# Twelve-head graph layers: the destination row is added inside PSUM by a K=3 bf16 matmul

## The reference, cut to what matters

```python
z   = (x @ W).reshape(N, 12, 64)
el  = sum(z * attn_l, axis=-1);  er = sum(z * attn_r, axis=-1)
e   = leaky_relu(el[src] + er[dst], 0.2)
ex  = exp(e - segment_max(e, dst)[dst])
out = segment_sum(ex / segment_sum(ex, dst)[dst] * z[src], dst) + z + bias
```

## Time and profile before

| what | value |
|---|---|
| runs | 3783.88 us median of 3 (3781.05, 3783.88, 3795.34) |
| span of the profiled execution | 3780.9 us |
| its own time | not listed apart; the fastest run, 3781.05 us, is 0.15 us above the span |
| PE busy, DVE busy, ACT busy | 2914.6 us (77%), 1979.8 us (52%), 1219.4 us (32%) |
| blocks of layer 0 | from 354.4 us to 825.3 us |
| blocks of layer 1 | from 1003.0 us to 1478.4 us |

### The profile page before, as it was taken

One profiled execution on the slowest core, in us unless ns is written; L12 is line 12 of the kernel. 1 busy time (PEld: TensorE's weight loads), 2 busy tenths in 40 slices (PEclk: granted clock), 3 DMA queues, 4 the chain that ended last, 5 costly groups with the idle time before them and its releaser, 6 DMA issues.

```text
span 3780.9 us, 46025 instructions
## 1 busy us (share of the span) xinstructions
PE 2914.6 (77%) x14456; PEld 2141.7 (57%) x14457; DVE 1979.8 (52%) x3392; ACT 1219.4 (32%) x1944; POOL 235.8 (6%) x267
## 2 busy tenths in 40 slices
PE   6874999978499996849369269649995994945995
PEld 4542888864288886425257124238884552534773
DVE  6745999945699984551431234556641434233113
ACT  1122778842277774230024101133320222001110
POOL 0000000000000000000001300000000000000112
PEclk9987999989799998979569679869997997965996
DMA  1011121121111212001335621122222100123435
GB/s 61 0 45 46 51 66 55 57 61 34 45 60 54 67 44 62 33 28 29 122 111 196 184 102 60 62 94 78 71 64 96 44 33 20 31 95 110 163 128 168
DMA packets 102475, 276.89 MB, mean 73 GB/s; under 512 B 25358, under 2 KB 38104, under 8 KB 99115
## 3 DMA queue, kind: packets, MB, share of 16 engines
q1 hardware_dynamic: 66794, 194.26, 14.1%
q0 software_dynamic: 32976, 73.59, 7.5%
q10 hardware_dynamic: 2600, 7.68, 0.5%
HBM read 204.99 MB, written 72.91 MB: 74 GB/s over the span
## 4 chain that ended last, share of the span: by engine, by line
PE 42%; DMA 13%; DVE 6%; issue 2%; ACT 1%; SPq 1%; POOL 1%; ACTq 0%; DVEq 0%; POOLq 0%
PE psum L914 16%; PE psum L870 12%; DMA arena<-raw 6%; PE psum L1032 4%; PE psum L1041 4%; PE psum L941 3%; DMA arena<-y_rows,arena 2%; PE psum L931 2%; DVE arena L1460 1%; DMA arena<-r_rows 1%; DMA arena<-xn_rows,arena 1%; PE psum L860 1%; DMA arena<-x 1%; DVE arena L1488 1%; DMA arena<-el_rows 1%
## 5 line engine op out<-in xcount | busy, mean ns | idle before, releaser
L914 PE MATMUL psum<-arena 125*125 125x256 f32 (+3 forms) x2400 | 626.1, 421 | 84.6 <-DVE arena L1490 84.6
L870 PE MATMUL psum<-arena 128*125 128x384 f32 (+1 forms) x1840 | 663.2, 520 | 0.0
L941 PEld LDWEIGHTS psum<-arena 125*125 125x125 f32 x4800 | 580.3, 191 | 71.7 <-DVE arena L1485 16.7
L914 PEld LDWEIGHTS psum<-arena 125*125 125x125 f32 x2400 | 449.5, 189 | 256.3 <-issue 66.9
L941 PE MATMUL psum<-arena 125*125 (+1 forms) x4800 | 568.3, 271 | 16.7 <-DVE arena L1485 16.6
L870 PEld LDWEIGHTS psum<-arena 128*125 128x125 f32 x1840 | 347.6, 191 | 291.2 <-issue 121.9
L1460 DVE CUSTOM_DVE_ANT_0 arena<-arena,no_edge_bias 125x1250 bf16<-125x1250 f32 x300 | 436.5, 1455 | 79.7 <-DMA arena<-el_rows 73.1
L931 PE MATMUL psum<-arena,spread 126*125 126x313 f32 (+1 forms) x1344 | 437.7, 449 | 33.4 <-DMA arena<-r_rows 18.7
L1485 DVE SCALAR_TENSOR_TENSOR arena<-arena,edge_counts 125x625 f32<-125x625 f32 x480 | 381.9, 805 | 79.5 <-ACT arena L1200 79.3
L1187 ACT ACTIVATE arena<-arena,el 125x625 f32<-125x625 f32 x480 | 386.4, 806 | 38.4 <-DMA arena<-el_rows 38.4
L1200 ACT ACTIVATE arena<-psum,el 125x625 f32<-125x625 f32 x336 | 262.6, 782 | 200.9 <-PE psum L931 179.2
(11 more groups left out here) (192 smaller groups left out, 2631.8 us busy)
## 6 DMA issues: line engine op xcount, KB each, us to landing
arena<-el_rows SPq DMA_DIRECT2D x54, 610.4 KB
arena<-in_L_ffn_W SPq DMA_DIRECT2D x16, 1152.0 KB, 9.1
y_rows<-arena SPq DMA_DIRECT2D x47, 384.0 KB, 2.4
arena<-raw SPq DMA_DIRECT2D x40, 375.0 KB
arena<-r_rows SPq DMA_DIRECT2D x24, 610.4 KB
arena<-in_L_w SPq DMA_DIRECT2D x16, 768.0 KB, 6.2
arena<-in_L_gnn_W SPq DMA_DIRECT2D x4, 3072.0 KB, 12.7
z_heads<-arena POOLq DMA_DIRECT2D x10, 1000.0 KB, 12.3
```

Of the source, the lines that this page charges most:

```text
L870: ins = e.matmul(bank[0:P, 0:w], L.xt[u][:, k, :], L.w_sb[:, k, at:at + w], start=(k == 0), stop=(k == L.KT - 1))
L914: ins = e.matmul(banks[2 + 2 * (j % 2) + c][0:P, 0:w], Ph[half][:, s, d * P:(d + 1) * P], (L.zh[u] if L.spill else L.z)[:, s, at:at + w], ...
L941: ins = e.matmul(banks[2 + half][0:P, d * 65:(d + 1) * 65], Ph[half][:, s, d * P:(d + 1) * P], L.z[:, s, h, :], start=(s == 0), stop=(s == ...
```

## The change

In the twelve-head layers:

- `relu` writes its block straight into PSUM (`block_exponents(j)`) for all 20 blocks, two blocks ahead instead of three; it waits until the exponential of block j - 2, ACT's own previous instruction but for a possible row copy, has finished, since there are only two such places.
- `exponents` adds the row to it there, `start=False`, with `ones3` (3 x 125, bf16) as the weights and three rows of bf16 as the moving side: the destination row is split into three bf16 parts whose sum is the f32 value. All 20 blocks go this way.
- `add_r2`, `rb2`, `r2`, `spread` and their semaphores go. `max_end` makes the three parts: seven small instructions in place of two. The transpose and the copy handle 30 columns instead of 20.
- SP's `lay_r3` writes the 30 x 125 bf16 rows to DRAM and reads them back as three rows (7.5 KB), where `lay_r2` had a 610 KB broadcast and six small reads. `load_el` follows directly.
- Four matmuls per layer write once over the four banks before the first block (`primed`).

```diff
-ADD_AT = [3, 7, 9]
...
-        spread = sb("spread", [P + 1, P])
+        ones3 = sb("ones3", [3, P], BF16)
+        r_part = sb("r_part", [P, 2 * 3 * T])
+        r_bf = sb("r_bf", [P, 2 * T], BF16)
...
-            def lay_r2(h, u, i, first, more):
+            def lay_r3(h, u, i):
 
                 e.wait_ge(L.rt_sb, L.since["rt_sb"] + h + 1)
                 apart(e)
-                e.dma_start(r_rows[h, T:2 * T, :], L.rt[u][T:2 * T, :]).then_inc(L.r_out[u], 16)
+                e.dma_start(r3_rows[h, :, :], L.rt3[u]).then_inc(L.r_out[u], 16)
                 e.wait_ge(L.r_out[u], L.since["r_out"][u] + 16 * (i + 1))
                 apart(e)
                 if not isinstance(i, int) or i > 0:
-                    e.wait_ge(L.added, L.since["added"] + ADDS * (h - 1))
+                    e.wait_ge(L.t_ready, L.since["t_ready"] + 2 * T * (h - 1))
                     apart(e)
-                e.dma_start(L.rb2[u], over(r_rows[h, T:2 * T, :].rearrange("t p -> (t p)"))).then_inc(L.rb2_in[u], 16)
-                for half in range(2):
-                    if not first:
-                        e.wait_ge(L.t_ready, L.since["t_ready"] + TURNS * (h - 1) + TURNS // 2 * (half + 1))
-                        apart(e)
-                    for v in range(3):
-                        e.dma_start(L.r2[half][P:P + 1, v, :],
-                                    r_rows[h, T + half * HT:T + (half + 1) * HT, :].rearrange("(o t) p -> o (t p)", o=1)
-                                    ).then_inc(L.r2_in[half], 16)
-                    if half == 0 and more:
-                        load_el(h + 2, u)
+                e.dma_start(L.r3[u], r3_rows[h, :, :].rearrange("(j t) p -> j (t p)", j=3)).then_inc(L.r3_in[u], 16)
...
                 def rows_of(h, u, i, more):
...
                     load_er(h, u)
-                    lay_r2(h, u, i, False, more)
+                    lay_r3(h, u, i)
+                    if more:
+                        load_el(h + 2, u)
...
-            def exponents(h, j):
+            def exponents(h, u, i, j):
 
                 half, s = j // T, j % T
-                if s == 0:
-                    e.wait_ge(L.r2_in[half], L.since["r2_in"][half] + 48 * (h + 1))
+                if j == 0:
+                    e.wait_ge(L.r3_in[u], L.since["r3_in"][u] + 16 * (i + 1))
                 e.wait_ge(L.relued, L.since["relued"] + 2 * T * h + j + 1)
-                e.wait_ge(L.e_ready, L.since["e_ready"] + 2 * T * h + j + 1)
                 o = block_exponents(j)
                 for at, to in ((0, CUT), (CUT, HALF)):
-                    ins = e.matmul(o[:, at:to], spread[:, :], L.r2[half][:, s % 3, at:to], start=True, stop=True)
+                    ins = e.matmul(o[:, at:to], ones3[:, :], L.r3[u][:, half * HALF + at:half * HALF + to],
+                                   start=False, stop=True, skip_group_check=True)
                 ins.then_inc(L.t_ready, 1)
...
-                    if s not in ADD_AT:
-                        exponents(h, j)
+                    exponents(h, u, i, j)
...
+            if L.batched:
+
+                for b in range(4, 8):
+                    ins = e.matmul(banks[b][0:P, 0:512], noti[:, :], MB[:, 0, 0:512], start=True, stop=True)
+                ins.then_inc(L.primed, 1)
...
-
+                e.wait_ge(L.e_ready, L.since["e_ready"] + 2 * T * h + j + 1)
                 apart(e)
-                e.activation(L.r2[half][0:P, s % 3, :], L.erb[u][:, half * HALF:(half + 1) * HALF], ACT.Relu,
+                e.activation(block_exponents(j), L.erb[u][:, half * HALF:(half + 1) * HALF], ACT.Relu,
                              bias=L.el8[:, s, bass.ds(h, 1)], scale=1.0 - SLOPE).then_inc(L.relued, 1)
...
-                e.activation(L.ex[j % 4], src, ACT.Exp, bias=L.el2[:, s, bass.ds(h, 1)]).then_inc(L.e_ready, 1)
+                e.activation(L.ex[j % 4], block_exponents(j), ACT.Exp, bias=L.el2[:, s, bass.ds(h, 1)]).then_inc(L.e_ready, 1)
...
-                    if j + 3 < 2 * T:
-                        relu(h, u, i, j + 3)
+                    if j + 2 < 2 * T:
+                        relu(h, u, i, j + 2)
...
+                if L.batched:
+                    q = r_part[:, u * 3 * T:(u + 1) * 3 * T].rearrange("p (j t) -> p j t", j=3)
+                    st.add(e.scalar_tensor_tensor(out=v[0], in0=er, scalar=SLOPE, in1=v[1], op0=ALU.mult, op1=ALU.subtract))
+                    st.wait()
+                    st.add(e.tensor_copy(r_bf[:, 0:T], v[0]))
+                    st.wait()
+                    st.add(e.tensor_copy(q[:, 0, :], r_bf[:, 0:T]))
+                    st.add(e.tensor_tensor(v[1], v[0], r_bf[:, 0:T], ALU.subtract))
+                    st.wait()
+                    st.add(e.tensor_copy(r_bf[:, T:2 * T], v[1]))
+                    st.wait()
+                    st.add(e.tensor_copy(q[:, 1, :], r_bf[:, T:2 * T]))
+                    e.tensor_tensor(q[:, 2, :], v[1], r_bf[:, T:2 * T], ALU.subtract).then_inc(L.r_ready, 1)
+                    return
                 st.add(e.tensor_tensor(r[:, 0:T], er, v[1], ALU.subtract))
...
-            def add_r2(h, u, i, j):
...
-                    if j + 3 < 2 * T and (j + 3) % T in ADD_AT:
-                        add_r2(h, u, i, j + 3)
```

More of the change, by code:

```diff
@@ L38 @@
 BAL_EPS = 0.01
-ADD_AT = [3, 7, 9]
-ADDS, TURNS = 2 * len(ADD_AT), 2 * (T - len(ADD_AT))
-def of_vector(j):
-    return sum(v % T in ADD_AT for v in range(j))
 def split(total, parts):
@@ L113, in __init__ @@
             elb_in=[16 * n for n in of], r_ready=heads, rt_ready=heads, rt_sb=heads, r_out=[16 * n for n in of],
-            rb_in=[16 * n * (not self.batched) for n in of], relued=2 * T * heads * self.batched, t_ready=TURNS * heads * self.batched,
-            added=ADDS * heads * self.batched, rb2_in=[16 * n * self.batched for n in of],
-            er_in=[16 * n * self.batched for n in of], r2_in=[48 * heads * self.batched] * 2, z_in=[16 * n * spill for n in of], e_ready=2 * T * heads, e_free=2 * T * heads * (not self.batched),
+            rb_in=[16 * n * (not self.batched) for n in of], primed=1 * self.batched, relued=2 * T * heads * self.batched, t_ready=2 * T * heads * self.batched,
+            er_in=[16 * n * self.batched for n in of], r3_in=[16 * n * self.batched for n in of], z_in=[16 * n * spill for n in of], e_ready=2 * T * heads, e_free=2 * T * heads * (not self.batched),
             p_ready=2 * T * heads, p_free=2 * heads, ag_ready=banks, out_done=banks, stored=[8 * banks] * 2)
@@ L128, in __init__ @@
         self.t_ready = signals["t_ready"]
-        self.added = signals["added"]
-        self.rb2_in = signals["rb2_in"]
+        self.primed = signals["primed"]
         self.er_in = signals["er_in"]
-        self.r2_in = signals["r2_in"]
+        self.r3_in = signals["r3_in"]
         self.x_in = signals["x_in"]
@@ L342, in graph_transformer @@
                 at += 2 * N
-                L.r2 = [carve(at + half * 3 * HALF, P + 1, 3 * HALF).rearrange("p (u d) -> p u d", u=3) for half in range(2)]
-                at += 6 * HALF
+                L.r3 = [carve(at + u * HALF, 3, HALF).bitcast(BF16) for u in range(2)]
+                at += 2 * HALF
                 L.ex = [carve(at + u * HALF, P, HALF) for u in range(4)]
@@ L348, in graph_transformer @@
                 at += 4 * HALF
-                L.rb2 = [carve(at + u * N, P, N) for u in range(2)]
-                at += 2 * N
+                L.rt3 = [carve(at + u * 63, 3 * T, 63).bitcast(BF16)[:, 0:P] for u in range(2)]
+                at += 126
             else:
@@ L569, in gat_sync @@
                 load_er(1, 1)
-                lay_r2(0, 0, 0, True, True)
-                lay_r2(1, 1, 0, False, True)
+                lay_r3(0, 0, 0)
+                load_el(2, 0)
+                lay_r3(1, 1, 0)
+                load_el(3, 1)
                 def rows_of(h, u, i, more):
@@ L945, in sum_tile, with batched_head @@
                     e.matmul(banks[1][0:1, 0:1], ident[:, 0:1], ident[:, 0:1], start=True, stop=True).then_inc(L.p_free, 1)
-            def batched_head(h, u, first, last):
+            def batched_head(h, u, i, first, last):
                 for j in range(2 * T):
                     half, s = j // T, j % T
-                    if s not in ADD_AT:
-                        exponents(h, j)
+                    exponents(h, u, i, j)
                     if not (first and half == 0):
@@ L1165, in rows @@
                 e.wait_ge(L.rt_ready, L.since["rt_ready"] + h + 1)
+                if L.batched:
+                    e.activation(L.rt3[u], banks[0][0:3 * T, 0:P], ACT.Copy).then_inc(L.rt_sb, 1)
+                    return
                 e.activation(L.rt[u], banks[0][0:2 * T, 0:P], ACT.Copy).then_inc(L.rt_sb, 1)
@@ L1206, in batched_head @@
                         rows(h + 1, 1 - u)
-                    if j + 3 < 2 * T:
-                        relu(h, u, i, j + 3)
+                    if j + 2 < 2 * T:
+                        relu(h, u, i, j + 2)
                     elif not last:
```

(15 more changed lines are left out.)

32 lines of the change are left out of this document (14 added, 18 removed).

## The result

The changed kernel takes **4306.48 us** (median of 4 runs, 4300.79 to 4311.25). The kernel before took 3786.35 beside it (4 runs, 3781.05 to 3795.34). The ratio is 1.136, with a 95% interval of 1.1333 to 1.1386: 13.6% slower where I forecast 3% faster. The profiled execution has a span of 4301.7 us, 520.8 above that of before.

The account below looks back on a forecast made before the run. The prediction took PE (37.2 us a head) as the bound, DVE close behind at 36.5; savings of 59 us per layer, 118 for two, less 7 in reserve, gave 3780.9 - 111 = 3669.9, so 3672 us, range 3648 to 3722.

Parts of the forecast that it names:

- the granted clock: PE in the twelve-head layers: clock 1.00 from head 1 on, so PE needs 28.4 us a head, behind DVE's 33.1.
- the rival on the other side: PE's new rests drop its clock to 1.2 GHz: 56.8 us a head, some 4200 us; 6% to end slower.
- The sign that I had named for it: Rows of L941, the sums, at 2.1 us in the middle of a layer would show the prediction wrong.
- A low clock makes PE the bound again, so its rests vanish: Argument against the low-clock rival: PE at the low level would set the pace and no longer rest.
- The window that was busy for 88% at 1.00: Argument against the low clock: the projection's window, PE busy 17.60 of 20 us, was granted 1.00 throughout.
- the 11.13 us of L941 alone: Argument against the low clock: at a layer's end, sums alone kept 0.11 us an instruction over 11 us.
- PE's pair: Per block on PE: two K=3 bf16 matmuls adding the row take 0.33 us beside sums of 1.07.
- ACT's wait on itself: Per block on ACT: the rectifier waits for the exponential just before it, 0.17 us more, block 1.55, head 31.3.
- ACT becomes the bound: Rival: ACT's wait of 0.35 us a block makes heads 34.9 us, 3719 us in all; 16% for 3692 to 3765.
- DVE and the heads: DVE sets heads 1 to 9 at 33.1 us, its 1.36 us wait for `el` gone; 0.3 per head kept back.
- The start: Layer start: row's write to first exponential takes 5.2 us, not 12.8; 6.6 us saved, head 0 another 3.4.
- The sum: Both layers: 59 us saved in each, 118, less 7 kept back, 111; forecast 3672 us, 3.0% less.

Follow-up runs that it names:

- e2: The changed kernel with the row matmul in f32 instead of bf16, still over 3 rows: 5076.27 us.
- e6: The changed kernel with extra unread matmuls of 3 rows, 512 columns, in head 0 of each layer, as many as in e3: 4374.3 us.
- e5: The changed kernel with the row matmul in f32 and over 125 rows, weights zero below the third: 3906.34 us.
- e3: The changed kernel with extra unread bf16 matmuls of 125 rows in head 0, eight for each of its first ten blocks, three for each of the last: 4294.18 us.
- e1: The changed kernel with the bf16 row matmul over 125 rows instead of 3, weights zero below the third: 4093.22 us.
- e4: The changed kernel, 3-row pairs kept, with two extra unread 125-row bf16 matmuls per block in all heads: 4643.84 us.
- f3: f1 with the row matmul left at 3 rows, same extra matmuls: 4314.18 us.
- f1: e1 plus extra 125-row matmuls: head 0 filled as in e3, 18 in head 1's first block, 8 at each later half: 3671.87 us, ratio 0.9715 to the kernel before.
- e12: e9 with the row matmul over 3 rows instead of 125: 3797.33 us.
- e9: e1 plus extra 125-row matmuls: e3's fill of head 0, 18 in head 1's first block, 5 at each half, 1 per other block: 3687.12 us.
- f2: f1 without the eight extra matmuls at each half from head 1 on: 4033.25 us.
- e7: e1 with e3's fill of head 0 and one extra 125-row matmul per block from head 1 on: 4272.94 us.
- e8: e1 with e3's fill of head 0 and no extra matmul from head 1 on: 4091.21 us.

## Why the prediction was wrong

**The step that failed is the granted clock.** The forecast priced PE at the full level, 28.4 us a head, and so put DVE in front; PE was at the low level in all of both layers' heads behind the first, took 60.45 us a head and set the time. I had this as the rival on the other side and gave it 6%. Its sum came close: 56.8 us a head and some 4200, measured 60.45 and 4306. The sign that I had named for it, sums of 2.1 us and more in the middle of a layer, is there (2.36 for ten at 625.65). Two arguments against it were wrong.

- "A low clock makes PE the bound again, so its rests vanish": they did vanish, and it changed nothing. PE was busy for 660 of 660 us at 0.50. Being busy isn't what brings the clock up; e2 and e6 are busy without a rest on 3 rows and stay low, e5 and e3 with 125 rows rise. That some full rows are there isn't enough either (e1, e4).
- The window that was busy for 88% at 1.00 and the 11.13 us of L941 alone were both of matmuls with 125 rows. They show such work at the full level. They say nothing of 3 rows, or of the way up. The same hundred sums alone, met at the low level, stayed there; timeline of PE in the changed kernel, end of layer 1:

```profile
1976.41 21.26 PE L928 MATMUL psum<-arena 125*125 125x65 f32 x100
```

The row that did bear on the way up was in the trace: the f32 L931 of 126 rows in head 0 (2.29 us, then 1.27).

The Trainium skill's section that I weighed, "A second HAM failure mode: psum-queue depth-cycling" in "TensorE: Matmul & The Clock Gate", expects a pace between the levels, up and down. The changed kernel doesn't go up and down: it is low for all of both layers. Only f3 alternates, and without any idle time of PE.

The other terms, read in the changed kernel and in f1, where the clock is full:

- **PE's pair.** I took 0.33 us beside ten sums of 1.07. At full clock a block with 3 rows is 401.54 - 399.90 = 1.64 us, not 1.40; with 125 rows it is 1.31 (f1, 621.67 to 622.98). A pair of 3 rows is 0.41 and delays the loads behind it. The bounds of a head (21.8 to 33.8) held it: 20 x 1.64 + 0.4 is 33.2. So even at full clock the 3-row form would have put PE level with DVE; that is an estimate from these rows, as no run has the 3-row form at full clock through a layer without an extra matmul per block. At the low level a block is 3.00 instead of 2 x 1.40 = 2.80; twenty times 0.20 is 4.0 us, and the head is 3.65 above my 56.8.
- **ACT's wait on itself.** Exponential to rectifier is 0.85 to 0.93 us (743.50 to 744.35 in f1, 370.39 to 371.31 above) where I had 0.84; rectifier to exponential is 0.73. Where ACT alone sets the pace in f1 its block is 744.35 - 742.77 = 1.58 (I had 1.55). The rival "ACT becomes the bound" didn't come about, though ACT (324.09 us busy) now stands beside DVE (321.24) in the window of f1.
- **DVE and the heads.** In f1 nine heads take (721.47 - 415.63) / 9 = 33.98 us, against 33.1 and the 0.3 kept back. Between 430 and 720 us DVE has no wait for `el`, and waits for ACT for 13.5 us in 22 places, about 1.6 a head, which neither list of mine held.
- **The start.** 5.27 us from write to first exponential, forecast 5.2. In f1 head 1's `turn_r` comes 425.88 - 415.63 = 10.25 us earlier than in the earlier trace rows, forecast 6.6 + 3.4 = 10.0.
- **The sum.** f1 takes 3671.87 us where I forecast 3672. Part of that is chance: f1 has padded rows and extra matmuls that my sum didn't. It shows that the relief of DVE and PE was there to be had with padded rows. From f1 to the changed kernel is 635 us. The clock is most of it but not all: at the same full clock 3 rows cost 110 us more than 125 (e12 - e9), so the forecast time isn't shown for the change as it was made.

**What stays open.** Whether the pause of 1.11 us or the thinner work cost f2 its clock, when the kernel before kept it behind pauses of 1.09 and 2.26 us. Whether it is the count of rows filled or a count of something that goes with it, as the zero weights below row 3 already suffice (e5); counts between 3 and 125 weren't tried. Which of f1's extra matmuls could still go; for the extra matmuls of a half only 0 (f2) and 8 were tried without others in the blocks. Why padded bf16 pairs hold the clock in f1 but don't bring it back in e1 and e7 is known only as a fact of these runs.

## What to carry to other kernels

Before a dense, full-row matmul is replaced by a thin one, find in the trace what brought the granted clock up after the last low stretch and ask whether that work is still there; a stage can run at half clock for its whole length with PE busy all the time. Read the clock beside the busy share in every window, and when it is low, try filling all rows (rows of zero weights saved 0.33 us a block at full clock here) and one burst of full-row matmuls where PE waits anyway. Then check the places where PE waits for another engine at each loop boundary, because behind a single pause the level can be gone for the rest of the layer (3.92 us in e8).

## What the runs showed of the hardware that I had not expected

- PE busy 660 of 660 us and 1050 of 1050 us (e2), and the granted clock 0.50 in all of it.
- Rows filled matter, at the same columns, type and count: 5076.27 us and low with 3, 3906.34 and full with 125 (e2, e5); 0.50 with 3, 0.96 with 125 (e6, e3). They aren't enough by themselves (e1, e4).
- The level depends on its history. The same block of work (padded pairs, ten sums, clean of extras) runs full through the blocks of f1 and low through e1, and a hundred sums alone take 11.13 us or 21.26.
- A pair of 3 rows in front of full-row matmuls isn't cheaper than one of 125: 0.41 us against 0.27 at full clock, 0.71 against 0.52 at the low one, as the weight loads behind it start late. In front of other 3-row matmuls it took 0.53 at the low level (e6, 381.56 to 382.09), so the loss lies in the change from 3 rows to 125. The Trainium skill, "TensorE: Matmul & The Clock Gate", section "Why this matters for your kernels", says that a single K=32 matmul takes as long as one of K=128; e6 agrees for K=3, and the pair in front of full-row matmuls took longer.
- ACT's wait on its own last result adds 0.18 to 0.26 us to the 0.67 of independent instructions.
